# Local attention layers: values projected token-major in full tiles, and carried by transfers into both copies

## What is computed

```python
def local_attention(q, k, v):
    nw = n // w                                   # w = 32, nw = 8 windows
    ...
    bk2, bv2 = (look(bk), look(bv))               # the window before and the own window
    sim = jnp.einsum('bhwie,bhwje->bhwij', bq, bk2) * QK_SCALE
    sim = jnp.where(mask, -jnp.finfo(sim.dtype).max, sim)
    attn = jax.nn.softmax(sim, -1)
    out = jnp.einsum('bhwij,bhwje->bhwie', attn, bv2)
def attn_layer(x, Wqkv, qs, ksc, Wo):
    qkv = x @ Wqkv                                # 128 -> 3 * 1024
    ...
for i in range(DEPTH):                            # DEPTH = 6
    x = attn_layer(shift_tokens(x), ...) + x
    x = ffn_layer(shift_tokens(x), ...) + x
```

## Time and profile before

| what | value |
|---|---|
| runs | 2818.03 us median of 3 (2814.33, 2818.03, 2821.95) |
| profiled execution, first to last instruction | 2820.1 us |
| TensorE busy | 2481.4 us, 88% |
| VectorE, ScalarE, GpSimd busy | 71%, 62%, 52% |
| mean granted TensorE clock | 0.942 of full speed |
| one pass of the local stage | 32.48 us |

### The profile page before, as it was taken

The page is one execution under the profiler, slowest core; times in us unless marked ns, Lnnn a source line. Parts: engine busy times, 40 slices in busy tenths (PEclk is TensorE's granted clock), DMA queues, the critical chain, the costliest instruction groups (busy, mean ns, idle before and its releaser), DMA issues. The chain is left out here.

```text
span 2820.1 us, 93390 instructions
## 1 busy us (share of the span) xinstructions
PE 2481.4 (88%) x35216; PEld 1693.3 (60%) x35244; DVE 2006.5 (71%) x3066; ACT 1754.3 (62%) x3659; POOL 1467.4 (52%) x1068
## 2 busy tenths in 40 slices
PE   7999858985647777589999999999999999999994
PEld 4777546664433344246666666666666666766663
DVE  5888653224218888768887888887888887888883
ACT  4666523333216777457777777777777777777773
POOL 2444223222124444366666666666666666666660
PEclk9999969998768999889999999999999999999997
DMA  9100016860410000111111112111211111121110
GB/s 333 35 0 0 20 34 169 233 189 25 132 38 1 0 0 0 53 28 27 26 48 41 39 26 56 34 26 41 58 30 26 48 41 28 37 56 34 26 26 29
DMA packets 124765, 147.61 MB, mean 52 GB/s; under 512 B 12240, under 2 KB 111632, under 8 KB 120336
## 3 DMA queue, kind: packets, MB, share of 16 engines
q1 hardware_dynamic: 120592, 138.22, 18.3%
q0 software_dynamic: 4096, 8.40, 1.0%
HBM read 75.27 MB, written 27.26 MB: 36 GB/s over the span
## 5 line engine op out<-in xcount | busy, mean ns | idle before, releaser
L2372 POOL TENSOR_TENSOR c<-a,bq 128x1024 f32<-128x1024 f32 x192 | 455.0, 2370 | 144.0 <-DVE bq L2437 129.6
L2033 PE MATMUL ps<-wqk,xs 128*128 128x512 f32 x768 | 372.3, 607 | 22.5 <-POOL xs L2365 17.8
L2382 POOL TENSOR_TENSOR qn<-c,ss 128x1024 f32<-128x1024 f32 x192 | 365.2, 1902 | 28.4 <-issue 3.4
L2436 DVE TENSOR_TENSOR a<-ps,tab 128x512 f32<-128x512 f32 x384 | 263.0, 685 | 83.4 <-ACT sq L2209 80.1
L2209 ACT ACTIVATE sq<-ps 128x512 f32<-128x512 f32 x384 | 224.5, 597 | 95.4 <-PE ps L2033 61.2
L2437 DVE TENSOR_TENSOR bq<-ps,tab 128x512 f32<-128x512 f32 x384 | 261.3, 681 | 0.0
L1425 POOL TENSOR_TENSOR hC<-hs,Cs 128x1024 f32<-128x1024 f32 x64 | 150.2, 2352 | 177.6 <-ACT Cs L1570 91.2
L2390 POOL TENSOR_TENSOR z<-z,sm 128x1024 f32<-128x1024 f32 x96 | 182.6, 1902 | 109.8 <-DVE sm L2465 99.1
L2444 DVE TENSOR_REDUCE ss<-sq 128x16 f32<-128x1024 f32 x192 | 230.3, 1199 | 3.9 <-POOL qn L2382 2.4
L2044 PEld LDWEIGHTS ps<-ident,qn 128*128 128x128 f32 x1536 | 173.1, 141 | 78.3 <-POOL qn L2382 40.6
L2033 PEld LDWEIGHTS ps<-wqk,xs 128*128 128x128 f32 x768 | 133.6, 192 | 128.6 <-issue 118.8
(11 more groups left out here) (313 smaller groups left out, 5759.3 us busy)
## 6 DMA issues: line engine op xcount, KB each, us to landing
Ve<-Vo SPq DMA_DIRECT2D x96, 256.0 KB, 4.3
Ve<-Vo SPq DMA_DIRECT2D x96, 192.0 KB, 4.4
win_rows<-rows_q SPq DMA_DIRECT2D x24, 256.0 KB, 3.3
outs_q<-win_out SPq DMA_DIRECT2D x24, 256.0 KB, 2.9
wqk<-in_wqkv SPq DMA_DIRECT2D x6, 1024.0 KB, 5.2
leaves<-in_f_w SPq DMA_DIRECT2D x9, 576.0 KB, 4.3
leaves<-in_q_w SPq DMA_DIRECT2D x1, 4608.0 KB, 18.8
leaves<-in_k_w SPq DMA_DIRECT2D x1, 4608.0 KB, 22.5
```

Of the source, the lines that this page charges most:

```text
L2033: nc.tensor.matmul(jobs.out(n), xs[:, t * 128:(t + 1) * 128], wqk[:, (2 * y + s) * 512:(2 * y + s + 1) * 512], start=True, stop=True).then ...
L2372: nc.gpsimd.tensor_tensor(f(c), f(a), f(bq), ALU.add).then_inc(c_ready.sem, 1)
L2382: nc.gpsimd.tensor_tensor(qn[:, t, y, :, :, :].rearrange("p h s e -> p h (s e)"), c[:, y, :, :, :].rearrange("p h s e -> p h (s e)"), spre ...
L2436: nc.vector.tensor_tensor(a[:, y, :, s, :], Zs, spread(table(0, s), H1), ALU.mult)
```

## The change

The tokens of a whole half (128) become the stationary operand of a full-tile matmul, and the result is token-major: `Vs[token in half, half, j, ...]`, j = 0 the even heads, j = 1 the odd heads. Four matmuls of 512 columns in place of eight half-width ones. ScalarE evicts the four banks into Vs. Then SyncE brings Vs into both Vo and Ve with twelve transfers in place of four. As Vo is now written by transfers, SyncE first waits for the four O jobs of the pass, and ScalarE's wait for O goes. The wait for `shared` ahead of take_values stays: it now keeps Vs from being overwritten while it is read.

```diff
+        Vs = sb("Vs3", [128, NT, 2, H1 // 2, E1])
...
-        SHARES = 4 * 16
+        SHARES = 12 * 16
+        VALUES = [f"O{t}.{j}" for t in range(NT) for j in range(2)]
...
                 def share_values(it):
 
+                    if not_first(it):
+                        for n in VALUES:
+                            sp.wait_ge(*jobs.filled(it, n))
+                            sp.sem_inc(sp_steps, 1)
                     sp.wait_ge(V_ready.sem, V_ready.at(it, 1))
-                    for p in (0, 64):
-                        sp.dma_start(Ve[p:p + W, :, :, :], Vo[p:p + W, :, :, :]).then_inc(shared, 16)
-                        sp.dma_start(Ve[p + W:p + 2 * W, 1:NG, :, :], Vo[p + W:p + 2 * W, 0:NG - 1, :, :]).then_inc(shared, 16)
+                    for j in range(2):
+                        p = 64 * j
+                        for c in range(2):
+                            sp.dma_start(Vo[p:p + 64, c::2, :, :], Vs[64 * c:64 * c + 64, :, j, :, :]).then_inc(shared, 16)
+                            sp.dma_start(Ve[p:p + W, c::2, :, :], Vs[64 * c:64 * c + W, :, j, :, :]).then_inc(shared, 16)
+                        sp.dma_start(Ve[p + W:p + 2 * W, 1::2, :, :], Vs[W:2 * W, :, j, :, :]).then_inc(shared, 16)
+                        sp.dma_start(Ve[p + W:p + 2 * W, 2, :, :], Vs[64 + W:64 + 2 * W, 0, j, :, :]).then_inc(shared, 16)
...
                 def project_values(it, half):
 
-                    for g in (2 * half, 2 * half + 1):
-                        n = f"V{g}"
+                    for j in range(2):
+                        n = f"V{2 * half + j}"
                         pe.wait_ge(*jobs.free(it, n))
-                        for p in (0, 64):
-                            last = nc.tensor.matmul(jobs.out(n)[p:p + 64, :], xs[:, g * 64:(g + 1) * 64],
-                                                    wv[:, p * 8:p * 8 + 512], start=True, stop=True, tile_position=(0, p))
-                        last.then_inc(jobs.sem_filled(n), 1)
+                        nc.tensor.matmul(jobs.out(n), xs[:, half * 128:(half + 1) * 128], wv[:, j * 512:(j + 1) * 512],
+                                         start=True, stop=True).then_inc(jobs.sem_filled(n), 1)
...
                 def take_values(it, half):
 
                     if not_first(it):
-                        act.wait_ge(*jobs.filled(it, f"O{half}.1"))
                         act.wait_ge(shared, it * SHARES)
-                    for g in (2 * half, 2 * half + 1):
-                        n = f"V{g}"
+                    for j in range(2):
+                        n = f"V{2 * half + j}"
                         act.wait_ge(*jobs.filled(it, n))
-                        nc.scalar.activation(Vo[:, g, :, :].rearrange("p m e -> p (m e)"), jobs.out(n), ACT.Copy)\
+                        nc.scalar.activation(Vs[:, half, j, :, :].rearrange("p m e -> p (m e)"), jobs.out(n), ACT.Copy)\
                             .then_inc(jobs.sem_drained(n), 1)
```

More of the change, by code:

```diff
@@ L1939, in local1 @@
         shared = core.sem("l1f_values_shared")
-        pe_steps, pool_steps = core.sem("l1f_pe_steps"), core.sem("l1f_pool_steps")
-        SHARES = 4 * 16
+        pe_steps, pool_steps, sp_steps = (core.sem(f"l1f_{e}_steps") for e in ("pe", "pool", "sp"))
+        SHARES = 12 * 16
+        VALUES = [f"O{t}.{j}" for t in range(NT) for j in range(2)]
         TURNS = {(0, 0): 0, (0, 1): 1, (1, 1): 2, (1, 0): 3}
```

## The result

The changed kernel takes 2835.68 us (median of 8 runs, 2829.47 to 2843.48), the kernel before 2821.59 in the same comparison (8 runs, 2814.33 to 2828.48): ratio 1.0047, 95% interval 1.0031 to 1.0064. By the ratio that is 13 us slower (9 to 18); the forecast was 20 slower. The profiled execution took 2833.83 us and spans 2832.0, 11.9 more than the span of before.

What follows compares the result with a forecast made beforehand. TensorE was taken to set the pace, with a 32.48 us iteration. Stalls of 41 us (25 ordinary, 13.5 layer ends, 2.5 last iteration) less 21.4 saved gave +20 on 2818.0: 2838 us (+0.7%), range 2805 to 2885.

Steps and rivals of the forecast that it cites:

- The forecast case: Shares land mildly late ahead of O0, L 11.4 to 12.5: chance 0.60, its own range 2810 to 2861 us.
- The projection: Value projection on TensorE: fewer changes of tile form save 0.45 us an iteration, 21.4 us over 48 iterations.
- The rival that it frees nothing on TensorE: Tile forms cost nothing by themselves, so the 0.45 is gone: 2859 us, counted in the upper range.
- ScalarE and SyncE's waits at nothing: Same four evictions and a dropped wait gain nothing on ScalarE; SyncE's four new waits for O0 and O1 are hidden.
- The time to the last landing, L = 12.0: Twelve share transfers, 1.97 MB: 12.0 us from first issue to last landing, between 10.7 and 13.0; before 6.4.
- ordinary stall: TensorE ahead of O0 in 40 ordinary iterations: waits 0.63 us each for the shares, 25 us.
- The layer ends: Five layer ends: value weights go ahead of the shares, which land 2.7 us too late each, 13.5 us.
- The last iteration: O0 comes 9.9 us behind the first share there, so it waits 2.5 us.
- 4.6 us for each 0.1: Sensitivity of kernel time to the shares' landing time L: every 0.1 us on L is 4.6 us.
- Hidden: Shares land by 11.4 us, so ordinary iterations don't stall and become 32.03; 2805 us at L = 10.7; chance 0.19.
- Issues in charge: SyncE's issues under traffic cost 0.98 us and more, setting L = 13.0 or more: 2883 us; chance 0.18.
- Transfers at the skill's rate: Shares land in 6.5 us by 2.0 us + bytes/436 GB/s, all hidden: 2797 us; chance 0.03.

Runs made afterwards that it cites:

- e1_tiles_only: Kernel before with only the full-tile projection, old eviction and four transfers, values in another order than the product reads: 2800.48 us, ratio 0.9917 to before.
- e3_two_shares: Changed kernel with shares split by token half, ten transfers sent early for O0, twelve later for O1, each with its own semaphore: 2798.22 us, ratio 0.9910 to before.
- e4_weights_behind: Changed kernel with the next layer's value weights issued behind the shares at a layer's last iteration, instead of ahead: 2818.37 us, ratio 0.9978 to before.
- e6_turn_about: Changed kernel with the same twelve transfers issued in turns into partitions 0 to 63 and 64 to 127: 2814.98 us, ratio 0.9987 to before.
- e7_more_bytes: Kernel before with each of its four transfers made twice, the second into a spare tile (1.84 MB, eight transfers, long rows): 2833.25 us, ratio 1.0061 to before.
- e8_small_transfers: Kernel before with nine 64 KB transfers into a spare tile added behind its four shares: 2836.36 us, ratio 1.0054 to before.
- e2_transfers_only: Changed kernel with the old half-width projection, keeping the new eviction, twelve transfers and waits: 2861.3 us, ratio 1.0129 to before.

## Why the prediction came out as it did

The forecast case was the right one (shares mildly late, O0 waits, the saved time behind O0), and so was the sign. Step by step:

**The projection, 0.45 a pass, 21.4 in all.** Right, slot by slot and as a sum: 0.45 in the kernel after, and shown alone by `e1_tiles_only` and `e3_two_shares`, whose pass is 32.03. The rival that it frees nothing on TensorE falls.

**ScalarE and SyncE's waits at nothing.** Right: ScalarE's busy time is the same to 1 us, and in `e3_two_shares` both edits stand and the pass has no stall.

**The time to the last landing, L = 12.0.** This is the term that was mis-sized. It measured 11.7, which is the slope between landings (11.8) without the addition for issues. The prediction had each issue under traffic cost 0.98 us, so that the last would start at 10.2; they cost 0.59 to 0.71, two of twelve 1.16 to 1.18, and the last starts at 8.6. The four old issues had grown to 0.98 and I carried that on as if it would stay. The ordinary stall is therefore 12.11 - 11.77 = 0.34 (0.36 in the median) and not 0.63: about 14 us in 40 passes where 25 were reckoned, and a pass that comes out 0.1 shorter than before instead of 0.1 to 0.2 longer. The 0.4 us from landing to O0 were right (0.41).

**The layer ends, 2.7 each, 13.5.** On the prediction's count, which sets them against a pass without any wait, they came to 13.4 + 5 x 0.36 = 15.2; near, but its make-up is another. The shares land 12.6 behind the first at most, not 13.5. The delay of O0 is 12.67 - 11.17 = 1.5, and 0.6 more since the first share goes out 0.97 behind the weights instead of 0.39: 2.1, not 2.7. The rest is the clock, whose fall at three of the five cost about 1.6 us each and which the prediction had not thought of. That the sum came out near is therefore luck: 0.6 too much per end for the landing, and 1.0 per end left out for the clock. `e4_weights_behind` shows that the order of weights and shares is the cause of the whole term beyond the ordinary wait.

**The last iteration, 2.5.** Right: 2.8.

On the prediction's count the terms measured are thus 14.4 + 15.2 + 2.8 - 21.6 = +10.8, against the spans' +11.9. Of the 20 us forecast the ordinary stall was 11 too high and the layer ends 2 too low. So the 0.3 us on L are the miss: at the prediction's own 4.6 us for each 0.1 they count for 14, and the clock, which it left out, gave 5 of them back.

**The rivals.** *Hidden* was near, as its turning point of L = 11.6 against 11.7 says: `e6_turn_about` needs 0.4 us less and loses the ordinary stall, though its 2815 us stay above the 2805 reckoned, for its layer ends. *Issues in charge* falls for this change: eight transfers with long rows (`e7_more_bytes`) and twelve with short ones land on one line by their bytes, and the last landing is 3.1 behind the last issue. It would be right for smaller transfers: in `e3_two_shares` and `e8_small_transfers` the issues set the landing. *Transfers at the skill's rate* falls too: the landings of 0.92 to 1.97 MB rise by 5.3 us for 1.05 MB, 198 GB/s. The Trainium skill (SBUF — State Buffer, The DMA port swizzle) gives 196 GB/s for a transfer of 1 MiB to partitions 0 to 63 and 189 for one to 0 to 31. The trace's 198 is near; it is the slope over several transfers, without the 1.7 us ahead of it, so the two are not quite the same quantity. The Trainium skill's sum of 2.0 us + bytes/436 GB/s (DMA: Bandwidth & Descriptors, Anatomy of one DMA), estimated at 6.5 us for these shares, is far from the measured 11.7. That section gives it for one transfer issued from GpSimd, so neither the four nor the twelve transfers of SyncE test it; the prediction read more into that disagreement than it holds.

**S1, 0.13 longer.** No step had it. It costs the kernel after nothing, since O0 waits for the shares anyway; it costs `e6_turn_about` 0.11 a pass, and the kernel would pay it if only the wait were cured.

## What to carry to other kernels

Work taken off the bound engine is kept only if no wait in the same loop grows with it: set the transfers' bytes over the rate that the trace shows against the slack of the first reader, before counting the gain. A transfer that is late need not be smaller or faster; it can be split by who reads it first, and the early part sent when it is ready (here the same bytes in 22 transfers cost 1 us, in 12 they cost 1.4%, by the ratios). Look at the places out of the ordinary too: a queue order that puts weights ahead of a transfer on the loop's path cost as much at five layer ends as the wait in forty ordinary passes.

## What the runs showed of the hardware

- TensorE's stream of small matmuls (S1, 130 records) goes from 1.73 us to 1.86 with two of the shares' issues under it (`after`), to 1.84 with issues under nearly all of it in `e6_turn_about` and to 2.00 in `e8_small_transfers`. Traffic alone (`e7_more_bytes`) leaves it at 1.74, and so do issues of weights under it. What in the issues of copies within the core's memory does it is open.
- A hole of TensorE of 1.7 to 2.2 us was followed by the lower clock level (0.50 of full speed for some 3 us) at three of five layer ends of the kernel after, at five of five in `e2_transfers_only`, and at one of five in `e7_more_bytes` (holes of 1.5 to 1.8); at none in `e6_turn_about` (1.1 to 1.7). The length of the hole doesn't separate the cases (2.03 without a fall, 1.66 with one), and no run settles what does.
- Transfers within one core's memory by one queue landed at 1.7 us + bytes / 196 GB/s for 0.92 to 1.97 MB in 4, 6, 8 and 12 transfers, while issues ran ahead of the data. Where they didn't, with transfers of 64 to 128 KB, the last one landed 2.0 to 2.1 us behind its issue, later than that line (8.9 for 1.05 MB, 11.1 for 1.51 MB). Alternating the destination's partition halves gained 0.4 us of 11.7.
- The issue of a share by SyncE took 0.59 to 0.71 us in four of five cases and up to 1.58 in the kernel after; it did not rise steadily as more were under way. With rows of 6 and 8 KB and eight transfers (`e7_more_bytes`) the median is 0.85.
